# The expert layer of a nine-layer kernel run as one sequence of 128 tiles

## The chip, the cores and the metric

One core of a Trainium2 chip runs the whole program once. The metric is the device time of an execution in microseconds (us). The engines are TensorE (PE in the profile; its weight loads are PEld), VectorE (DVE), ScalarE (ACT), GpSimd (POOL) and SyncE (SP).

## The reference

Input x of 8 x 256 tokens of 128 features goes through four blocks: a block with two quantised attentions and a gated feed-forward, a masked cross attention with a feed-forward, a cross attention, and a decoder block with self attention, cross attention and eight experts. All is float32. The change is in the experts, the last of the nine layers:

```python
def _moe(x, rw, rb, w1, b1, w2, b2):
    ...
    xf = x.reshape(T, D)
    router_weights = jax.nn.softmax(xf @ rw + rb, axis=-1)
    topw, topi = jax.lax.top_k(router_weights, K)          # K = 2 of E = 8
    topw = jax.nn.softmax(topw, axis=-1)
    combine = jnp.zeros((T, E), xf.dtype).at[jnp.arange(T)[:, None], topi].add(topw)
    h = jax.nn.gelu(jnp.einsum('td,edf->etf', xf, w1) + b1[:, None, :], approximate=False)
    eo = jnp.einsum('etf,efd->etd', h, w2) + b2[:, None, :]
    out = jnp.einsum('etd,te->td', eo, combine)
...
x = _layernorm(x + _moe(x, router_w, router_b, e_w1, e_b1, e_w2, e_b2), ln3_g, ln3_b)
```

Every token goes through all eight experts (D = 128, FF = 512), and `combine` weighs them.

## The kernel before

Each engine runs a program of its own, in an order written out by hand; semaphores tie them together. The expert layer takes 2048 tokens as four chunks of 512. A chunk has 32 tiles: tile k is one quarter (128 rows) of the hidden layer of expert k // 4. Float32 is kept by splitting each operand into two float16 parts, hi and lo.

- TensorE, `up` (L1123 to L1125): three matmuls of 512 columns (hi x hi, hi x lo, lo x hi) into one of four PSUM banks. `down` (L1142 to L1144): for each of four token groups three matmuls of 128 columns, gathered over the four tiles of an expert in one of two banks (`TP`). The down of tile k is issued after the up of tile k + 2.
- ScalarE: gelu from the bank to `U_full` in float32 (L1490) and, for three tiles in four, a second pass of the same to the float16 hi part (L1493). Tile k uses slot k % 4.
- VectorE, `split`: the hi part as a cast for k % 4 = 1 (L1962, `HI_BY_VECTOR`), and lo = u - hi for each tile (L1964). `take` (L1974) adds an expert's result, weighed by `combine_down`, to the residual X in four instructions.
- Side work of a chunk. TensorE: transposes of the next chunk's tokens (L1053), the router's matmuls (L1151), the transposes of `combine` (L1159) and the matmuls of the experts' bias (L1165). VectorE: the router's softmax and top 2 as some 24 small dependent instructions (`routing`, parts 0 to 5), statistics and application of the norm for the next chunk (L1515, L1519, L1525) and of the last norm for the chunk before, the tokens and their two float16 parts (`tokens`, `token_parts`), the bias addition (`add_bias`, L1982). GpSimd: two powers for the router (L2449, `route_exp`), inverse deviations (L2196, L2198), scale and shift of the norms (`base` L2205, L2211; `finish` L2386, L2389).
- The token parts have one buffer, rewritten for the next chunk when the last up of the chunk has been issued. The router of the next chunk waits for `routed` 3c + 3, which is the bias addition of this chunk, since both use the PSUM tensor `CO`.

On TensorE and VectorE chunk 0 and chunk 3 are written out and chunks 1 and 2 are a loop; on ScalarE chunks 1 to 3 are a loop. GpSimd's program is written out. GpSimd has also split the expert weights in an earlier layer (L2439).

## Time and profile before

| what | value |
|---|---|
| median of 3 runs | 1049.2 us (1048.2 to 1049.9) |
| the profiled execution's own time | 1049.15 us |
| span of the profile, first to last instruction | 1047.4 us |
| mean granted TensorE clock | 0.862 |
| busy in the span | PE 83%, DVE 73%, ACT 58%, POOL 50% |
| the expert layer's first up | 824.3 us from the span's start |
| its last up matmul | starts at 1034.2 us |

Busy shares are means over nine layers with different limits. For a change in one layer, the layer's own windows and waits are read. A busy time is the union of the records of an engine; records of neighbouring instructions overlap a little, so the distance from a start to the next start is what an instruction costs in a queue.

### The profile page before, as it was taken

To read this page: it belongs to the slowest core of one execution; us is meant where nothing else is said; L and a number is where in the kernel's file an instruction comes from. 1 tells how busy PE (TensorE), PEld (TensorE's weight loads), DVE (VectorE), ACT (ScalarE), POOL (GpSimd) and SP (SyncE) were. 2 spreads that over 40 slices of the span, in tenths; PEclk is the share of its full clock that TensorE was granted. 3 is DMA by queue.
4 is the path that set the end of the run, shared out by engine and by line. 5 is a ranking of instruction groups with operands and counts; after the bars stand their busy time and mean duration, and the time that the engine had idled before them with its cause. 6 is when DMAs were issued, how large, how long until landed. Compare 5 with 4: busy or idle time off the path is not lost.

```text
span 1047.4 us, 23536 instructions
## 1 busy us (share of the span) xinstructions
PE 867.2 (83%) x8314; PEld 528.5 (50%) x8314; DVE 763.5 (73%) x1680; ACT 612.3 (58%) x1487; POOL 519.7 (50%) x1045
## 2 busy tenths in 40 slices
PE   3798888974555877998999799998988788888895
PEld 1344444442333554555765456565555466565664
DVE  5788888978775664565567667677477788989886
ACT  0777777858885313544355456654555566666674
POOL 2677777776563323763444465655244222333313
PEclk9995555555555989999999899999999999999998
DMA  8400000000000000000000010000000000000000
GB/s 266 150 1 2 0 0 1 1 2 0 1 2 0 2 0 1 2 2 2 1 2 2 20 27 22 25 23 15 2 2 2 1 1 2 2 12 0 10 2 21
DMA packets 23573, 16.39 MB, mean 16 GB/s; under 512 B 8744, under 2 KB 20400, under 8 KB 23344
## 3 DMA queue, kind: packets, MB, share of 16 engines
q1 hardware_dynamic: 23472, 15.06, 5.0%
q8 instruction: 61, 1.00, 0.4%
q14 instruction: 40, 0.33, 0.1%
HBM read 10.85 MB, written 1.05 MB: 11 GB/s over the span
## 4 chain that ended last, share of the span: by engine, by line
PE 49%; DVE 25%; ACT 9%; issue 9%; POOL 6%; DMA 1%; DVEq 1%; SPq 0%; ACTq 0%; POOLq 0%
ACT sb_E L1239 5%; PE ps_context L780 5%; DVE sb_neg_raw L1536 3%; PE ps_context L783 3%; POOL sb_E L2261 3%; PE ps_scores L856 3%; DVE sb_E L1964 3%; PE ps_scores L880 3%; DVE sb_inv_den L1779 2%; PE ps_scores L733 2%; PE ps_scores L773 2%; PE ps_turned L1084 2%; PE ps_scores L674 2%; DVE sb_neg_half L1747 2%; PE ps_turned L694 2%
## 5 line engine op out<-in xcount | busy, mean ns | idle before, releaser
L1239 ACT ACTIVATE sb_E<-ps_scores,sb_neg_max,sb_score_scale 128x256 f32<-128x256 f32 (+1 forms) x384 | 190.9, 515 | 64.0 <-DVE sb_neg_max L1539 63.6
L2261 POOL TENSOR_SCALAR sb_E<-sb_E,sb_inv_sum 128x256 f16<-128x256 f32 x256 | 123.6, 483 | 47.3 <-DVE sb_inv_sum L1576 29.5
L1490 ACT ACTIVATE sb_E<-ps_scores,sb_ff_bias 128x512 f32<-128x512 f32 x128 | 87.6, 688 | 66.6 <-PE ps_scores L1125 64.4
L1142 PE MATMUL ps_turned<-sb_moe_down,sb_E 128*128 128x128 f16 x512 | 92.6, 220 | 23.9 <-DVE sb_E L1964 23.8
L1964 DVE TENSOR_TENSOR sb_E<-sb_E 128x512 f16<-128x512 f32 x128 | 93.1, 745 | 23.4 <-ACT sb_E L1493 21.2
L1536 DVE TENSOR_REDUCE sb_neg_raw<-ps_scores 128x4 f32<-128x1024 f32 (+1 forms) x80 | 97.4, 1218 | 14.4 <-PE ps_scores L674 12.0
L1747 DVE TENSOR_REDUCE sb_neg_half<-ps_scores 128x16 f32<-128x1024 f32 x48 | 58.7, 1223 | 67.1 <-PE ps_scores L856 67.1
L1559 DVE TENSOR_REDUCE sb_neg_quad<-ps_scores 128x2 f32<-128x512 f32 (+1 forms) x96 | 64.5, 685 | 42.2 <-PE ps_scores L735 30.1
L1144 PE MATMUL ps_turned<-sb_moe_down,sb_E 128*128 128x128 f16 x512 | 92.1, 219 | 0.0
L1143 PE MATMUL ps_turned<-sb_moe_down,sb_E 128*128 128x128 f16 x512 | 92.1, 219 | 0.0
L2196 POOL TENSOR_SCALAR sb_veps<-sb_mv 128x2 f32<-128x2 f32 x72 | 17.3, 240 | 148.2 <-DVE sb_mv L1519 144.4
L1265 ACT ACTIVATE sb_E<-ps_scores 128x512 f32<-128x512 f32 x96 | 57.0, 598 | 47.7 <-PE ps_scores L775 46.5
L674 PE MATMUL ps_scores<-sb_KBD,sb_QS 32*128 32x512 f16 x128 | 64.2, 602 | 23.5 <-ACT sb_E L1239 15.8
L694 PEld LDWEIGHTS ps_turned<-sb_ident,sb_E 128*128 128x128 f16 x640 | 66.6, 143 | 32.8 <-issue 16.3
L694 PE MATMUL ps_turned<-sb_ident,sb_E 128*128 128x128 f16 x640 | 80.8, 304 | 0.3 <-issue 0.2
L1362 ACT ACTIVATE sb_E<-ps_scores 128x1024 f32<-128x1024 f32 x48 | 49.2, 1024 | 54.5 <-PE ps_scores L888 54.5
L1239 ACT ACTIVATION_READ_ACCUMULATOR sb_E<-ps_scores,sb_neg_max,sb_score_scale 128x1 f32 x384 | 79.7, 207 | 0.0
L1142 PEld LDWEIGHTS ps_turned<-sb_moe_down,sb_E 128*128 128x128 f16 x512 | 50.2, 98 | 50.1 <-DVE sb_E L1964 33.8
L1586 DVE TENSOR_SCALAR sb_VCTX<-ps_turned 128x1024 f16<-128x1024 f16 x80 | 53.7, 672 | 24.6 <-PE ps_turned L694 24.2
L1493 ACT ACTIVATE sb_E<-ps_scores,sb_ff_bias 128x512 f16<-128x512 f32 x96 | 65.4, 681 | 0.0
L2211 POOL TENSOR_TENSOR sb_X<-sb_X,sb_rows 128x256 f32<-128x256 f32 (+1 forms) x64 | 48.1, 752 | 28.7 <-DVE sb_z L1525 26.2
L1779 DVE RECIPROCAL sb_inv_den<-sb_raw_context 128x256 f32<-128x256 f32 x32 | 55.8, 1744 | 4.2 <-ACT sb_raw_context L1370 4.2
(285 smaller groups left out, 2257.2 us busy)
## 6 DMA issues: line engine op xcount, KB each, us to landing
sb_moe_up<-in_moe_up SPq DMA_DIRECT2D x1, 2048.0 KB
sb_KS<-sb_qk_parts SPq DMA_DIRECT2D x96, 16.0 KB, 1.8
sb_QS<-sb_qk_parts SPq DMA_DIRECT2D x96, 16.0 KB, 1.8
sb_rows<-in_rows SPq DMA_DIRECT2D x1, 1216.0 KB, 7.5
out_x<-sb_raw_context SPq DMA_DIRECT2D x8, 128.0 KB, 1.8
sb_X<-in_x SPq DMA_DIRECT2D x1, 768.0 KB, 9.5
sb_square<-in_square SPq DMA_DIRECT2D x1, 768.0 KB, 11.0
sb_ctxT<-in_ctxT SPq DMA_DIRECT2D x1, 512.0 KB, 11.2
```

The costliest lines, as they stand in the source:

```text
L674: last = pe.matmul(dst[:, h:h + 512], QS[group, b, 0, tile:tile + P], KBD[group, b, h:h + 512], start=True, stop=True)
L694: last = pe.transpose(dst[:, P * k:P * k + P], E16[:, ring, P * k:P * k + P], ident16[:, :])
L1142: pe.matmul(dst, u_hi, hi, start=(first and i == 0), stop=False, skip_group_check=True)
L1143: pe.matmul(dst, u_hi, lo, start=False, stop=False, skip_group_check=True)
L1144: last = pe.matmul(dst, u_lo, hi, start=False, stop=final_, skip_group_check=True)
L1239: last = act.activation(E[:, ring, head], SC[t % 2][:, head], ACT.Exp, bias=neg_max[:, ring, h:h + 1], scale=scale, accum_out=row_sum[:, r ...
L1490: last = act.activation(U_full[:, k % 4, :], banks[k % 4], ACT.Gelu, bias=bias, scale=1 / WEIGHT_SCALE)
L1536: dve.tensor_reduce(neg_raw[:, ring, 0:L.heads], src, AX.X, ALU.max).then_inc(S["raw_max"], 1)
L1747: dve.tensor_reduce(neg_half[:, n % 2, :, :, :].rearrange("p x i g -> p (x i g)"), SC[0][:, :].rearrange("p (h k) -> p h k", k=CTX), AX.X, ...
L1779: dve.reciprocal(inv_den[:, :], raw_context[:, x % 2, SEQ:2 * SEQ]).then_inc(S["den_ready"], 1)
L1964: dve.tensor_tensor(lo, u, hi, ALU.subtract).then_inc(S["split"], 1)
L2261: last = pool.tensor_scalar(E16[:, ring, SEQ * h:SEQ * h + SEQ], E[:, ring, SEQ * h:SEQ * h + SEQ], inv_sum[:, ring, h:h + 1], HALF, ALU.m ...
```

## The change

The 128 tiles of the four chunks become one written-out sequence. The down of tile n is issued after the up of tile n + 4 (`BEHIND`), also across chunks. The activations have eight slots (`RING`), the token parts two buffers. Every fourth lo part (k % 4 = 3) is computed by GpSimd (`lower`), with a semaphore of its own. The side work is at other tiles: takes a tile later, the transposes of `combine` from tile 16 to 11, the bias matmuls from 22 to 16, the transposes of the next tokens from 26 to 18, the router from 30 to 25, the bias addition from 27 to 25; statistics and norms one batch at a time; token parts in two steps at tiles 22 and 23; the last norm of the chunk before at tiles 17, 18 (statistics) and 29, 30 (application), where it was at 16 and 20. The buffers are places in tensors that earlier layers have left. The diff, cut to what matters:

```diff
-HI_BY_VECTOR = 1
+HI_BY_VECTOR, LO_BY_POOL = 1, 3
+BEHIND, RING = 4, 8
...
-        h_parts = KBD[:, 0, 0:2 * CHUNK].rearrange("p (s k) -> p s k", s=2)
-        U_parts = E16[:, :, :].rearrange("p r (s k) -> p r s k", s=2)
+        h_parts = KBD[:, 0, 0:4 * CHUNK].rearrange("p (b s k) -> p b s k", b=2, s=2)
+        U_parts = (*(E16[:, i, :] for i in range(4)), *(KBD[:, 1, UNIT * i:UNIT * i + UNIT] for i in range(4)))
         up_parts = moe_up[:, :, :].rearrange("p e k -> p (e k)").bitcast(F16).rearrange("p (e k) -> p e k", e=EXPERTS)
         down_parts = moe_down[:, :, :, :].rearrange("p e t d -> p (e t d)").bitcast(F16)\
             .rearrange("p (e k) -> p e k", e=EXPERTS)
-        U_full = E[:, 2:4, :].rearrange("p r (s k) -> p (r s) k", s=2)
-        final_z = E[:, 0, 0:4 * D].rearrange("p (u t d) -> p u t d", u=2, t=2)
+        U_full = E[:, :, :].rearrange("p r (s k) -> p (r s) k", s=2)
+        final_z = V32[:, 0, :, :, :].rearrange("p t h c -> p (t h c)")[:, 0:4 * D].rearrange("p (u t d) -> p u t d", u=2, t=2)
...
+                    pe.matmul(dst, hi, h_parts[:, c % 2, 0, :], start=True, stop=False)
+                    pe.matmul(dst, hi, h_parts[:, c % 2, 1, :], start=False, stop=False)
+                    pe.matmul(dst, lo, h_parts[:, c % 2, 0, :], start=False, stop=True).then_inc(S["up"], 1)
...
-                    wait(pe, S["split"], B["split"] + n + 1)
+                    if k % 4 == LO_BY_POOL:
+                        pe.wait_ge(S["split_p"], B["split_p"] + n // 4 + 1)
+                    else:
+                        pe.wait_ge(S["split"], B["split"] + n - n // 4 + 1)
...
-                def chunk(c, following):
-                    for k in range(L.tiles):
-                        if not (isinstance(c, int) and c == 0 and k < 2):
-                            up(c, k)
-                        if k == 16:
-                            turn_combine(c)
-                        if k == 22:
-                            expert_bias(c)
-                        if k == 26 and following:
-                            chunk_turn(L, B, c + 1)
-                        if k == 30 and following:
-                            router(c + 1)
-                        if k > 1:
-                            down(c, k - 2)
-                    down(c, L.tiles - 2)
-                    down(c, L.tiles - 1)
+                def tile(n):
+                    c, k = divmod(n, L.tiles)
+                    if n >= 2:
+                        up(c, k)
+                    if k == 11:
+                        turn_combine(c)
+                    if k == 16:
+                        expert_bias(c)
+                    if k == 18 and c < NCHUNK - 1:
+                        chunk_turn(L, B, c + 1)
+                    if k == 25 and c < NCHUNK - 1:
+                        router(c + 1)
...
+                for n in range(NCHUNK * L.tiles + BEHIND):
+                    if n < NCHUNK * L.tiles:
+                        tile(n)
+                    if n >= BEHIND:
+                        down(*divmod(n - BEHIND, L.tiles))
...
+                for n in range(NCHUNK * L.tiles):
+                    k = n % L.tiles
+                    act.wait_ge(S["up"], B["up"] + n + 1)
+                    if n >= RING:
+                        act.wait_ge(S["down"], B["down"] + n - RING + 1)
+                    bias = ff_bias[:, 12 + k:13 + k]
+                    last = act.activation(U_full[:, n % RING, :], banks[n % 4], ACT.Gelu, bias=bias, scale=1 / WEIGHT_SCALE)
+                    if k % 4 != HI_BY_VECTOR:
+                        last = act.activation(U_parts[n % RING][:, 0:CHUNK], banks[n % 4], ACT.Gelu, bias=bias,
                                               scale=1 / WEIGHT_SCALE)
-                        if k % 4 != HI_BY_VECTOR:
-                            last = act.activation(U_parts[:, k % 4, 0, :], banks[k % 4], ACT.Gelu, bias=bias,
-                                                  scale=1 / WEIGHT_SCALE)
-                        last.then_inc(S["act"], 1)
...
-                    wait(dve, S["up"], B["up"] + L.tiles * c)
+                    if c > 1:
+                        dve.wait_ge(S["up"], B["up"] + L.tiles * (c - 1))
                     dve.wait_ge(S["hT_part"], B["hT_part"] + 2 * c + 1)
-                    dve.tensor_copy(h_parts[:, 0, :], h).then_inc(S["hT_part"], 1)
+                    dve.tensor_copy(h_parts[:, c % 2, 0, :], h).then_inc(S["hT_part"], 1)
+                def token_rest(c):
                     dve.wait_ge(S["hT_part"], B["hT_part"] + 2 * c + 2)
-                    dve.tensor_tensor(h_parts[:, 1, :], h, h_parts[:, 0, :], ALU.subtract).then_inc(S["chunk_hT"], 1)
+                    dve.tensor_tensor(h_parts[:, c % 2, 1, :], h, h_parts[:, c % 2, 0, :], ALU.subtract)\
+                       .then_inc(S["chunk_hT"], 1)
                 def split(c, k):
                     n = L.tiles * c + k
                     dve.wait_ge(S["act"], B["act"] + n + 1)
-                    u, hi, lo = U_full[:, k % 4, :], U_parts[:, k % 4, 0, :], U_parts[:, k % 4, 1, :]
+                    u, hi, lo = U_full[:, n % RING, :], U_parts[n % RING][:, 0:CHUNK], U_parts[n % RING][:, CHUNK:]
                     if k % 4 == HI_BY_VECTOR:
                         dve.tensor_copy(hi, u).then_inc(S["u_hi"], 1)
-                        dve.wait_ge(S["u_hi"], B["u_hi"] + L.tiles // 4 * c + k // 4 + 1)
+                        dve.wait_ge(S["u_hi"], B["u_hi"] + n // 4 + 1)
                     dve.tensor_tensor(lo, u, hi, ALU.subtract).then_inc(S["split"], 1)
...
-                def chunk(c, following):
-                    ended = not isinstance(c, int) or c > 0
-                    for k in range(L.tiles):
-                        if k == 28 and following:
-                            tokens(c + 1)
-                        if k == L.tiles - 1 and following:
-                            token_parts(c + 1)
+                def tile(c, k):
+                    following, ended = c < NCHUNK - 1, c > 0
+                    if k % 4 != LO_BY_POOL:
                         split(c, k)
-                        if k == 8 and following:
-                            next_stats(B, c)
-                        if k == 12 and following:
-                            next_norms(B, c)
-                        if k == 30 and following:
-                            routing(c + 1, 0)
-                        if k in (2, 3, 4, 5):
-                            routing(c, k - 1)
-                        if k == 7:
-                            routing(c, 5)
-                        if k == 16 and ended:
-                            final_stats(c - 1)
-                        if k == 20 and ended:
-                            final_norms(c - 1)
-                        if k == 18:
-                            dve.wait_ge(S["logits"], 3 * c + 2)
-                            dve.tensor_copy(combineT[:, :], CO[0:EXPERTS, :]).then_inc(S["routed"], 1)
-                        if k % 4 == 3 and k > 3:
-                            take(c, k // 4 - 1)
-                        if k == 27:
-                            add_bias(c)
-                    take(c, EXPERTS - 1)
+                    if k in (0, 4) and ended:
+                        take(c - 1, EXPERTS - 2 + k // 4)
+                    if k % 4 == 0 and k > 4:
+                        take(c, k // 4 - 2)
+                    if k in (2, 3, 4, 5):
+                        routing(c, k - 1)
+                    if k == 7:
+                        routing(c, 5)
+                    if k in (9, 10) and following:
+                        norm_stats(B, 2 * c + 2 + k - 9, k - 9)
+                    if k == 13:
+                        dve.wait_ge(S["logits"], 3 * c + 2)
+                        dve.tensor_copy(combineT[:, :], CO[0:EXPERTS, :]).then_inc(S["routed"], 1)
+                    if k in (14, 15) and following:
+                        wait(dve, S["x_based"], B["x_based"] + 2 * c + 1 + k - 14)
+                        norm_apply(B, 2 * c + 2 + k - 14, k - 14)
+                    if k in (17, 18) and ended:
+                        final_stats(c - 1, k - 17)
+                    if k == 21 and following:
+                        tokens(c + 1)
+                    if k == 22 and following:
+                        token_parts(c + 1)
+                    if k == 23 and following:
+                        token_rest(c + 1)
+                    if k == 25:
+                        add_bias(c)
+                    if k == 27 and following:
+                        routing(c + 1, 0)
+                    if k in (29, 30) and ended:
+                        final_norms(c - 1, k - 29)
...
+                def lower(n):
+                    u, hi, lo = U_full[:, n % RING, :], U_parts[n % RING][:, 0:CHUNK], U_parts[n % RING][:, CHUNK:]
+                    pool.wait_ge(S["act"], B["act"] + n + 1)
+                    pool.tensor_tensor(lo, u, hi, ALU.subtract).then_inc(S["split_p"], 1)
+                route_exp(0, route[:, 1, :], route[:, 2, :], EXP1)
                 for c in range(NCHUNK):
-                    route_exp(c, route[:, 1, :], route[:, 2, :], EXP1)
-                    route_exp(c, route_s[:, 4, :], route_s[:, 5, :], EXP2)
-                    if c + 1 < NCHUNK:
-                        chunk_norms(L, B, c + 1)
+                    for k in range(LO_BY_POOL, L.tiles, 4):
+                        if k == 7:
+                            route_exp(c, route_s[:, 4, :], route_s[:, 5, :], EXP2)
+                        if k == 11 and c < NCHUNK - 1:
+                            for b in range(2):
+                                inverse_std(B, 2 * c + 2 + b, b)
+                        lower(L.tiles * c + k)
+                        if k == 15 and c < NCHUNK - 1:
+                            for b in range(2):
+                                base(L, B, 2 * c + 2 + b, b)
+                        if k == 19 and c > 0:
+                            final_inverses(c - 1)
+                        if k == 27 and c < NCHUNK - 1:
+                            route_exp(c + 1, route[:, 1, :], route[:, 2, :], EXP1)
                     if c > 0:
                         finish(c - 1)
+                final_inverses(NCHUNK - 1)
                 finish(NCHUNK - 1)
```

## Rows read from the trace of the kernel before

**Rows 1.** The page's part 1, busy time of each engine.

```profile
PE 867.2 (83%) x8314; PEld 528.5 (50%) x8314; DVE 763.5 (73%) x1680; ACT 612.3 (58%) x1487; POOL 519.7 (50%) x1045
```

**Rows 2.** Windows of the expert layer, one row for each chunk.

```profile
core 0: us, PE busy (x) PEld busy (x) DVE busy (x) ACT busy (x) POOL busy (x), PEclk, DMA share, GB/s
...
878.70:933.10 54.40, 46.89 (x509) 32.67 (x507) 47.34 (x128) 35.64 (x56) 19.09 (x19) 1.00 0.02 6
...
987.40:1034.60 47.20, 43.57 (x472) 29.98 (x469) 40.06 (x106) 34.39 (x54) 11.25 (x10) 1.00 0.03 7
```

**Rows 3.** Timeline of TensorE, one tile in step (start, length, line).

```profile
891.55 0.38 PE L1123 MATMUL ps_scores<-sb_KBD,sb_moe_up 128*128 128x512 f16 x1
...
892.20 0.22 PE L1142 MATMUL ps_turned<-sb_moe_down,sb_E 128*128 128x128 f16 x1
...
892.87 0.38 PE L1123 MATMUL ps_scores<-sb_KBD,sb_moe_up 128*128 128x512 f16 x1
```

**Rows 4.** Timeline of TensorE at the router's matmuls.

```profile
928.12 1.05 PE L1151 MATMUL ps_context<-sb_router_w,sb_hT 128*128 128x8 f32 x8 [0.99 <-DVE sb_hT L1945]
929.03 0.22 PE L1142 MATMUL ps_turned<-sb_moe_down,sb_E 128*128 128x128 f16 x1
```

**Rows 5.** Groups of TensorE in chunk 1 (busy us, mean ns, idle before).

```profile
L1165 PE MATMUL ps_context<-sb_moe_b,sb_combineT 8*128 8x128 f32 x8 | 1.2, 283 | 0.0
...
L1053 PE MATMUL ps_rounds<-sb_ident,sb_z 128*128 128x128 f32 x4 | 0.6, 272 | 0.0
```

**Rows 6.** Waits in chunk 1 (us in total, times, longest).

```profile
PE ps_turned L1142 <- DVE sb_E L1964: 7.3, 8, 1.4
...
DVE sb_E L1964 <- ACT sb_E L1493: 4.1, 6, 1.1
```

**Rows 7.** Timeline of all engines, the last tile.

```profile
1034.19 0.38 PE L1125 MATMUL ps_scores<-sb_KBD,sb_moe_up 128*128 128x512 f16 x1
...
1035.19 0.68 ACT L1493 ACTIVATE sb_E<-ps_scores,sb_ff_bias 128x512 f16<-128x512 f32 x1
...
1035.90 0.69 DVE L1964 TENSOR_TENSOR sb_E<-sb_E 128x512 f16<-128x512 f32 x1 [1.22 <-ACT sb_E L1493]
```

**Rows 8.** Timeline of VectorE, chunk 0: routing begins; tiles 24 and 25.

```profile
831.99 0.18 DVE L2042 RECIPROCAL sb_route_s<-sb_route_s 128x4 f32<-128x4 f32 x1
832.20 0.19 DVE L2043 TENSOR_TENSOR sb_route<-sb_route,sb_route_s 128x32 f32<-128x32 f32 x1
...
866.41 0.68 DVE L1964 TENSOR_TENSOR sb_E<-sb_E 128x512 f16<-128x512 f32 x1
867.01 0.42 DVE L1962 CAST sb_E<-sb_E 128x512 f16<-128x512 f32 x1
```

**Rows 9.** VectorE's lo part L1964: the page, then the line's own view.

```profile
L1964 DVE TENSOR_TENSOR sb_E<-sb_E 128x512 f16<-128x512 f32 x128 | 93.1, 745 | 23.4 <-ACT sb_E L1493 21.2
...
L1964 DVE TENSOR_TENSOR sb_E<-sb_E x128: 670/692/1214, 827.9 to 1035.9; 128x512 f16<-128x512 f32 x128
```

**Rows 10.** Groups of VectorE in chunk 1.

```profile
L1519 DVE BATCH_NORM_AGGREGATE sb_mv<-sb_bn 128x2 f32<-128x6 f32 x8 | 1.0, 166 | 0.6 <-DVE sb_bn L1515 0.6
```

**Rows 11.** GpSimd's powers of the router, the line's own view.

```profile
L2449 POOL TENSOR_TENSOR sb_route_s<-sb_euler,sb_route_s x4: 1006/1258/1512, 837.4 to 998.6; 128x4 f32<-128x4 f32 x4
```

**Rows 12.** Timeline of ScalarE, first gelu of chunk 2.

```profile
934.45 0.69 ACT L1490 ACTIVATE sb_E<-ps_scores,sb_ff_bias 128x512 f32<-128x512 f32 x1 [2.64 <-PE ps_scores L1125]
```

**Rows 13.** GpSimd's weight splits L2439, the line's own view.

```profile
L2439 POOL TENSOR_TENSOR sb_moe_up<-sb_act_g,sb_moe_up x8: 1151/1158/1165, 419.7 to 571.4; 128x512 f16<-128x512 f32 x8
```

**Rows 14.** Timeline of VectorE beside GpSimd's residual operations.

```profile
903.06 3.37 DVE L1964 TENSOR_TENSOR sb_E<-sb_E 128x512 f16<-128x512 f32 x3
```

**Rows 15.** Groups of GpSimd before the expert layer (410 to 820 us).

```profile
L2211 POOL TENSOR_TENSOR sb_X<-sb_X,sb_rows 128x256 f32<-128x256 f32 x32 | 23.2, 726 | 4.1 <-DVE sb_z L1525 2.7
```

**Rows 16.** Window of chunk 0 from routing to tile 25.

```profile
831.80:867.00 35.20, 31.13 (x336) 21.30 (x334) 29.96 (x82) 24.13 (x38) 7.98 (x9) 1.00 0.01 1
```

**Rows 17.** Timeline of GpSimd, the last inverse deviations.

```profile
1039.76 0.22 POOL L2196 TENSOR_SCALAR sb_veps<-sb_mv 128x2 f32<-128x2 f32 x1 [15.18 <-DVE sb_mv L1519]
```

More of the change, by code:

```diff
@@ L276, in counts @@
         if layer.experts > 1:
-            c.update(hT_part=2 * NCHUNK, u_hi=n // 4, split=n, chain=NCHUNK * layer.chain, routed=NCHUNK * 3, route_exp=NCHUNK * 2, logits=NCHUNK * 3)
+            c.update(hT_part=2 * NCHUNK, u_hi=n // 4, split=n // 4 * 3, split_p=n // 4, chain=NCHUNK * layer.chain, routed=NCHUNK * 3, route_exp=NCHUNK * 2, logits=NCHUNK * 3)
         return c
@@ L1140, in down @@
                         dst = TP[e % 2][:, P * i:P * i + P]
-                        u_hi, u_lo = (U_parts[:, k % 4, part, P * i:P * i + P] for part in range(2))
+                        u_hi, u_lo = (U_parts[n % RING][:, CHUNK * part + P * i:CHUNK * part + P * i + P] for part in range(2))
                         pe.matmul(dst, u_hi, hi, start=(first and i == 0), stop=False, skip_group_check=True)
@@ L1204, in experts @@
                         plan_step(layer, step)
-                chunk(0, True)
-                with pe.Fori(1, NCHUNK - 1) as c:
-                    chunk(c, True)
-                chunk(NCHUNK - 1, False)
+                for n in range(NCHUNK * L.tiles + BEHIND):
[3 more added lines that the diff above has]
+                        down(*divmod(n - BEHIND, L.tiles))
             pe.wait_ge(loaded["a"], N_LOADS["a"])
@@ L1482, in experts @@
                     act.wait_ge(S[s], B[s])
-                def chunk(c):
-                    for k in range(L.tiles):
-                        n = L.tiles * c + k
-                        act.wait_ge(S["up"], B["up"] + n + 1)
-                        wait(act, S["down"], B["down"] + n - 3)
-                        bias = ff_bias[:, 12 + k:13 + k]
-                        last = act.activation(U_full[:, k % 4, :], banks[k % 4], ACT.Gelu, bias=bias,
-                                              scale=1 / WEIGHT_SCALE)
-                        if k % 4 != HI_BY_VECTOR:
-                            last = act.activation(U_parts[:, k % 4, 0, :], banks[k % 4], ACT.Gelu, bias=bias,
-                                                  scale=1 / WEIGHT_SCALE)
-                        last.then_inc(S["act"], 1)
-                chunk(0)
-                with act.Fori(1, NCHUNK) as c:
-                    chunk(c)
+                for n in range(NCHUNK * L.tiles):
[7 more added lines that the diff above has]
+                        last = act.activation(U_parts[n % RING][:, 0:CHUNK], banks[n % 4], ACT.Gelu, bias=bias,
+                                              scale=1 / WEIGHT_SCALE)
+                    last.then_inc(S["act"], 1)
             act.wait_ge(setup_v, V_SETUP)
@@ L1926, in next_norms, with final_stats, final_norms @@
                     norm_apply(B, 2 * c + 2 + b, b)
-            def final_stats(c):
+            def final_stats(c, b):
                 wait(dve, S["taken"], BASE[-1]["taken"] + EXPERTS * (c + 1))
-                for b in range(2):
-                    norm_stats(Counter(), 2 * c + b, b, sems=fin)
-            def final_norms(c):
-                for b in range(2):
-                    dve.wait_ge(fin["scaled"], 2 * c + b + 1)
-                    norm_apply(Counter(), 2 * c + b, b, sems=fin, z=final_z)
+                norm_stats(Counter(), 2 * c + b, b, sems=fin)
+            def final_norms(c, b):
+                dve.wait_ge(fin["scaled"], 2 * c + b + 1)
+                norm_apply(Counter(), 2 * c + b, b, sems=fin, z=final_z)
             def experts(L, B):
@@ L1979, in add_bias @@
                     dve.wait_ge(S["logits"], 3 * c + 3)
-                    wait(dve, S["taken"], B["taken"] + EXPERTS * c + 6)
+                    wait(dve, S["taken"], B["taken"] + EXPERTS * c + 5)
                     x = chunk_of_x(c)
@@ L2076, in head @@
                         token_parts(c)
+                        token_rest(c)
                     if k == "first":
@@ L2085, in experts @@
                         plan_step(layer, step)
-                chunk(0, True)
-                with dve.Fori(1, NCHUNK - 1) as c:
-                    chunk(c, True)
-                chunk(NCHUNK - 1, False)
-                final_stats(NCHUNK - 1)
-                final_norms(NCHUNK - 1)
+                for c in range(NCHUNK):
+                    for k in range(L.tiles):
+                        tile(c, k)
+                for e in (EXPERTS - 2, EXPERTS - 1):
+                    take(NCHUNK - 1, e)
+                for b in range(2):
+                    final_stats(NCHUNK - 1, b)
+                for b in range(2):
+                    final_norms(NCHUNK - 1, b)
             def chain(sem):
```

9 lines of the change are left out of this document (4 added, 5 removed).

## The prediction

> **What bounds the kernel now.** I read the page first. TensorE is busy 83% of the span and VectorE 73%, so neither is a bound by itself [rows 1]. The diff touches only the expert layer, so the rest of the reading is of that layer. The windows cut it into its four chunks: the first three take 54.4, 54.4 and 54.3 us, the last 47.2, all at a granted clock of 1.00 (the second and the last stand in [rows 2]). In a middle chunk VectorE is busy 47.3 us and idle 7.1; TensorE is busy 46.8, idle 7.5; ScalarE 35.6 and GpSimd 19.1 lie far below. The chunk is longer than either of its two busy engines: they wait for each other in turn.
>
> The timeline of TensorE shows what it needs when nothing is late: from one tile's first up matmul (891.55) to the next (892.87) are 1.32 us, 0.65 for the three ups and 0.67 for the twelve downs [rows 3]. 32 tiles are 42.2 us. Its side work adds about 2.9 us: router 0.91 (928.12 to 929.03), bias matmuls 1.1, two groups of transposes 0.45 each, by issue [rows 4, 5]. So TensorE's floor is 45.1 us a chunk, 9.3 below what it takes.
>
> The waits of a middle chunk say where this goes: TensorE waits for VectorE's lo part (L1964) 7.3 us in 8 places, VectorE for ScalarE 4.1 us in 6 [rows 6]. A down follows its up by only two tiles: from the start of a tile's last up matmul TensorE has 0.22 + 0.67 + 0.65 + 0.67 + 0.65 = 2.9 us of other matmuls before that tile's down. The path through the other engines is: up matmul at 1034.19, second gelu pass ends 1035.87, lo from 1035.90 to 1036.59 [rows 7], 2.4 us. That leaves 0.4 us. Any take (four instructions, 1.04 us) or group of routing links overruns it. Then TensorE stands, its next up is late, and VectorE stands for that up.
>
> **Where the chain goes after the change.** Downs four tiles behind and eight slots let VectorE run 2 x 1.32 = 2.6 us later than now (3.0 in place of 0.4) without stopping TensorE. A short overrun is then absorbed, and the average decides: TensorE's 45.1 against VectorE's load. I make that load from the 47.3 busy of now, term by term.
>
> 1. One lo in four leaves VectorE: 8 of 32 per chunk, each 0.60 us from its start to the next start (866.41 to 867.01 in [rows 8]; the record itself is 0.69 [rows 9]). 47.3 - 4.8 = 42.5. The casts, takes, statistics, norms, links, token parts and bias are the same instructions at other tiles: nothing.
> 2. Gaps that stay: 0.6 between statistics and their aggregate [rows 10], and about 1.0 in some 30 dependent links (0.21 apart at 0.18 busy [rows 8]). 1.6.
> 3. The second exp of the router: GpSimd needs 1.26 in the median [rows 11]. Now two lo parts stand in that gap, afterwards one, since tile 7's lo is GpSimd's. 0.75.
> 4. A wait that moves. The router's matmuls go from tile 30 to 25, and they wait for the bias addition (same PSUM bank, "routed" 3c+3), which goes from 27 to 25. Three tiles of distance become none. At tile 25 TensorE issues the up, then stands until gelu (starts 0.42 after the last up matmul starts [rows 7], one pass, 0.69), cast 0.45, lo 0.60 and addition 0.69 are done: 2.8 us. Behind the router in its queue are down 21 and up 26, so ScalarE and VectorE then find nothing. From the addition's end: router 0.97, down 0.67, two up matmuls 0.43, 0.42 to gelu, two gelu passes 1.27: VectorE idles 3.8 us per chunk. This is the largest price of the change.
> 5. What goes: the stop at the chunk's end. Now the only token buffer is rewritten at tile 31 and TensorE waits for it; ScalarE stood 2.64 us before the next chunk's first gelu [rows 12]. With two buffers this is gone. It is not a term, it is part of the idle time that I don't carry over.
> 6. GpSimd's lo: 128x512 f16 from f32, 1.158 us, in the weight splits, which have exactly this form (8 of the 16 stand in [rows 13]). Eight are 9.3 us a chunk; on 19.1 busy it has room. But it gets in VectorE's way. From 903.06 three lo parts took 3.37 us [rows 14], where 0.60 + 0.60 + 0.69 = 1.9 is the undisturbed time; GpSimd then ran its four 128x256 additions and multiplications of the residual. Over the layer, the mean lo is 745 ns against a median of 692 [rows 9]: 53 ns x 128 = 6.8 us lost. GpSimd has six such groups of four in the layer before the last up, 24 x 0.726 [rows 15] = 17.4 us: 0.39 per us of GpSimd. So 0.45 per moved lo. The bounds: 0 when it runs in VectorE's own gap (tile k%4 = 3 has no lo on VectorE, and in step that leaves 1.3 us for 1.16), and 1.16 when VectorE is behind and always wants the operands. I take 0.45 for six of eight; those of tiles 27 and 31 follow the stop at 25, when VectorE has no backlog. 2.7.
>
> The Trainium skill (SBUF — State Buffer, section "SBUF: two separate sides") says that the pair of ports that VectorE and GpSimd share is an exclusive lock, held for the whole instruction, and that a VectorE instruction with two SBUF inputs takes part in it. The 3.37 us for three agree with it. By that rule a lag on VectorE makes each GpSimd lo cost its full 1.158, which would make rival C of the forecast.
>
> Sum of VectorE's chain: 42.5 + 1.6 + 0.75 + 3.8 + 2.7 = 51.35 us per chunk; TensorE's: 45.1 + 2.8 = 47.9. VectorE sets it, 2.95 below 54.3.
>
> **The sum along the kernel.** Now, VectorE reaches tile 25's cast in chunk 0 at 867.0; its routing of that chunk goes on from 831.8 (the second link after the exp is at 831.99 in [rows 8]). Between, it is busy 30.0 of 35.2 [rows 16]. Six lo parts go (-3.6), tokens and token parts come before tile 25 (+1.8), of 5.2 idle I keep 1.7 (-3.5), contention 6 x 0.45 (+2.7): 864.4, the addition ends 1.75 later, 866.1. Two periods: 968.8. From there no router follows, and TensorE's own chain is the longer: 1.64 to up 26, 37 tiles of 1.32, 0.43, side work 1.6: last up matmul at 1021.3, now 1034.2, so 12.9 us earlier. Tail: the last lo is GpSimd's (+0.56), and the norms of chunk 2 sit at tiles 29, 30, so GpSimd's four multiplications and additions of them (some 3 us) stand before the inverse deviations of chunk 3, which start at 1039.8 now, 5.6 us after the last up matmul [rows 17]: 1.0 late in all. Net 11.9. The profiled execution's own time is 1049.15 (span 1047.4 and 1.75 around it), the median of the runs 1049.2: 1049.15 - 11.9 = **1037.2 us**.
>
> Covered at nothing: other slots in other tiles and unrolled loops (chunk 0 is unrolled and chunk 1 a loop, both 54.4); ScalarE's waits, since it is idle a third of a chunk. Cover for GpSimd's queue: its lo 11 stands behind the inverse deviations of tile 10, about 0.7 to 1.3 us before down 11 needs it; its lo 31 behind the 5.44 us exp. If VectorE is over 1 us behind, TensorE waits there, which costs only what VectorE doesn't have as backlog.
>
> **Rivals.**
> A, TensorE paces: GpSimd's lo falls in VectorE's gaps and costs nothing. Periods of 47.9, chunk 0's addition at 863.4: last up at 1011.7, 22.5 earlier, net 21.5: 1027.7. For it: the gap at every fourth tile. Against: tiles 4 to 7 load VectorE with 7.1 us (three lo parts 1.8, cast 0.45, take 1.04, 14 links 3.1, the wait of term 3) against TensorE's 5.3, and start a lag. 25%.
> B, little is left: contention of about 0.8 on each of the 22 GpSimd lo parts up to tile 25 of chunk 2, 17.6 us where the forecast has 8.1: 1046.7, from 1043 to 1050; or TensorE kept by late GpSimd parts (exp, inverse deviations) while VectorE has no backlog, some 3 us a chunk, to the same sum. For it: the whole routing of tiles 2 to 7 has short instructions that a GpSimd lo of 1.16 can each stop. 19%.
> C, slower: the ports are held for all of each GpSimd lo. Periods 48.65 + 9.3 = 57.9, chunk 0's addition at 870.4, the last part paced by VectorE too (57): last up at 1043, net 10 later: 1059. It decides from about 0.91 us lost per lo, where the 11.9 us are used up (22 x 0.91 = 8.1 + 11.9). Against it: 0.39 per us measured. 8%.
> D, it does not do what it says: TensorE still stops at nearly each take, because up n still needs gelu n-4 (four banks), and the time is as now. Against: by the path above that gelu ends 2.1 us after its up's start, and up n starts 5.3 us after it. 3%.
> Forecast: 45%, own range 1031 to 1043.
>
> **Numbers.** No change is within 0.2% (2.1 us), which is about what the measurement of this kernel can tell. Faster: forecast, A and most of B, 0.87. Same: the end of B and D, 0.05. Slower: C and edges, 0.08. The range runs from A with a somewhat shorter tail (1025) to B with late GpSimd parts (1048).
>
> **What would show it.** Right: middle chunks of 51 to 52 us; one gap of TensorE of 2.8 us or more at the router, once per chunk, and a VectorE gap near 3.8 behind it; no pair of gaps at the chunk's end; the mean VectorE lo above 0.75; 32 GpSimd lo parts between 1.16 and 1.7. Wrong: chunks near 48 with VectorE idle at each fourth tile (A); VectorE lo parts over 0.9 in the mean (B, C); waits of TensorE for GpSimd's lo (B); TensorE waiting for VectorE in eight places a chunk (D).

## The result and the profile after

The changed kernel takes 1061.1 us (median of 4 runs, 1060.6 to 1061.3), the kernel before beside it 1048.7: a ratio of 1.0115, with a 95% interval of 1.010 to 1.013. It is slower by 12 us. The prediction was 1037.2, 12 faster, and the measured time lies outside its range; "slower" had a chance of 0.08.

The windows of the changed kernel, cut at the up of tile 25 of each chunk (columns as in [rows 2]):

```profile
core 0: us, PE busy (x) PEld busy (x) DVE busy (x) ACT busy (x) POOL busy (x), PEclk, DMA share, GB/s
...
864.70:923.50 58.80, 50.60 (x508) 36.61 (x506) 43.25 (x114) 35.91 (x57) 25.12 (x23) 0.91 0.01 1
923.50:981.50 58.00, 49.04 (x508) 35.08 (x506) 45.48 (x118) 35.88 (x57) 29.57 (x27) 0.94 0.02 6
981.50:1045.20 63.70, 56.21 (x593) 40.41 (x591) 46.79 (x119) 42.26 (x67) 24.70 (x20) 0.95 0.02 6
```

A chunk has grown from 54.3 us to 58.8 and 58.0. VectorE is busy 43.3 and 45.5 us of it, about the 45.2 that the forecast gives it (42.5 + 2.7). But it is idle 12.5 to 15.5 us, where the forecast has 6. And the granted clock of TensorE, 1.00 in every chunk before, is 0.91 to 0.95. The waits of the first of these windows show whom TensorE waits for, to be set against [rows 6]:

```profile
PE ps_context L1155 <- DVE sb_X L1983: 4.2, 1, 4.2
...
PE ps_context L1163 <- DVE sb_combine L2073: 1.5, 1, 1.5
...
PE ps_turned L1146 <- POOL sb_E L2467: 1.4, 1, 1.4
...
PE ps_context L1169 <- DVE sb_combineT L2003: 0.9, 1, 0.9
...
PE ps_turned L1146 <- DVE sb_X L1975: 0.2, 1, 0.2
```

The eight short waits for VectorE's lo part are gone, as the deeper sequence promised. In their place stand four long ones, of which three are side work: the router (L1155) for the bias addition, the transposes of `combine` (L1163) for `combine`, the bias matmuls (L1169) for its copy, and one down (L1146) for GpSimd's lo. Around the first router, on TensorE and on VectorE:

```profile
864.68 0.38 PE L1124 MATMUL ps_scores<-sb_KBD,sb_moe_up 128*128 128x512 f16 x1
...
869.70 1.85 PE L1155 MATMUL ps_context<-sb_router_w,sb_hT 128*128 128x8 f32 x8 [4.21 <-DVE sb_X L1983]
871.40 0.27 PE L1146 MATMUL ps_turned<-sb_moe_down,sb_KBD 128*128 128x128 f16 x1
...
872.63 0.63 PE L1124 MATMUL ps_scores<-sb_KBD,sb_moe_up 128*128 128x512 f16 x1
...
875.20 0.63 PE L1124 MATMUL ps_scores<-sb_KBD,sb_moe_up 128*128 128x512 f16 x1
```

```profile
864.72 1.53 DVE L1954 TENSOR_TENSOR sb_KBD<-sb_hT,sb_KBD 128x512 f16<-128x512 f32 x1
866.17 0.68 DVE L1965 TENSOR_TENSOR sb_E<-sb_E 128x512 f16<-128x512 f32 x1
866.78 1.12 DVE L1975 SCALAR_TENSOR_TENSOR sb_X<-ps_turned,sb_combine_down,sb_X 128x128 f32<-128x128 f32 x4
867.81 0.41 DVE L1963 CAST sb_E<-sb_E 128x512 f16<-128x512 f32 x1
868.26 0.69 DVE L1965 TENSOR_TENSOR sb_E<-sb_E 128x512 f16<-128x512 f32 x1
868.87 0.68 DVE L1983 TENSOR_TENSOR sb_X<-ps_context,sb_X 128x512 f32<-128x512 f32 x1
875.53 0.69 DVE L1965 TENSOR_TENSOR sb_E<-sb_E 128x512 f16<-128x512 f32 x1 [5.97 <-ACT sb_E L1494]
```

Between the up of tile 25 (864.68) and that of tile 26 (872.63) are 8.0 us, between 26 and 27 another 2.6, where 1.32 is the pace [rows 3]. TensorE stands 4.2 us; then everything that it does takes twice as long: the router 1.70 from start to next start (0.91 in [rows 4]), an up matmul's record 0.63 (0.38), the down 1.23 (0.67). VectorE, which TensorE has waited for, gets its next lo at 875.53, after 6.0 us of idle. The clock in that stretch:

```profile
865.00:868.00 3.00, 0.49 (x3) 0.00 (x0) 3.00 (x7) 1.17 (x2) 0.70 (x1) 1.00 0.00 0
868.00:869.00 1.00, 0.00 (x0) 0.00 (x0) 0.97 (x3) 0.00 (x0) 0.00 (x0) 1.00 0.00 0
869.00:870.00 1.00, 0.30 (x2) 0.33 (x2) 0.55 (x1) 0.00 (x0) 0.00 (x0) 0.66 0.00 0
870.00:876.00 6.00, 6.00 (x37) 4.67 (x37) 0.47 (x1) 1.27 (x2) 0.00 (x0) 0.50 0.01 3
876.00:877.00 1.00, 1.00 (x15) 0.83 (x14) 0.70 (x4) 0.49 (x1) 0.00 (x0) 0.93 0.00 0
```

It falls from 2.4 to 1.2 GHz at about 869.3, near the end of the gap, and returns at about 876.1.

### The profile page after: what moved, and what is told of

It reads as the page before. It is cut to its first block, busy times and chain, and to the rows that moved or that the text cites. A ratio compares the mean times of both kernels' runs of the same rounds, so it can differ in the third digit from the quotient of the medians.

```text
span 1059.4 us, 23096 instructions
## 1 busy us (share of the span) xinstructions
PE 874.6 (83%) x8314; PEld 536.4 (51%) x8314; DVE 755.1 (71%) x1648; ACT 612.4 (58%) x1487; POOL 558.7 (53%) x1077
## 4 chain that ended last, share of the span: by engine, by line
PE 48%; DVE 27%; issue 9%; ACT 9%; POOL 6%; DMA 1%; DVEq 0%; SPq 0%; POOLq 0%; ACTq 0%
ACT sb_E L1241 5%; PE ps_context L781 5%; DVE sb_neg_raw L1534 3%; PE ps_context L784 3%; POOL sb_E L2271 3%; PE ps_scores L857 3%; PE ps_scores L881 3%; DVE sb_inv_den L1777 2%; DVE sb_X L1975 2%; PE ps_scores L734 2%; PE ps_scores L774 2%; PE ps_turned L1085 2%; PE ps_scores L675 2%; DVE sb_neg_half L1745 2%; PE ps_scores L1069 1%
## 5 line engine op out<-in xcount | busy, mean ns | idle before, releaser
L1965 DVE TENSOR_TENSOR sb_E<-sb_E 128x512 f16<-128x512 f32 x48 | 38.4, 808 | 26.6 <-ACT sb_E L1494 25.7
L2208 POOL TENSOR_TENSOR sb_rstd<-sb_veps,sb_minus_half 128x2 f32<-128x2 f32 x72 | 53.1, 738 | 6.0
L1146 PE MATMUL ps_turned<-sb_moe_down,sb_KBD 128*128 128x128 f16 x256 | 50.2, 230 | 2.0 <-DVE sb_X L1975 1.0
L1146 PE MATMUL ps_turned<-sb_moe_down,sb_E 128*128 128x128 f16 x256 | 46.2, 219 | 5.7 <-POOL sb_E L2467 4.3
L1148 PE MATMUL ps_turned<-sb_moe_down,sb_KBD 128*128 128x128 f16 x256 | 50.2, 230 | 0.0
L1147 PE MATMUL ps_turned<-sb_moe_down,sb_KBD 128*128 128x128 f16 x256 | 50.2, 230 | 0.0
```

The costliest lines, as they stand in the source:

```text
L1146: pe.matmul(dst, u_hi, hi, start=(first and i == 0), stop=False, skip_group_check=True)
```

## The experiments

All are edits of the changed kernel, timed beside the kernel before in several rounds. Ratios are to the kernel before.

### The bias addition earlier, alone

```diff
-                    wait(dve, S["taken"], B["taken"] + EXPERTS * c + 5)
+                    wait(dve, S["taken"], B["taken"] + EXPERTS * c + 3)
...
-                    if k == 25:
+                    if k == 19:
                         add_bias(c)
```

> The bias addition of a chunk goes from tile 25 to tile 19 (it then waits for three takes, not five); all else is as in the changed kernel. Theory S (the router's matmuls stop TensorE at tile 25 because the addition that they wait for has the same tile; the step from up 25 to up 26 is 8.0 us, the next 2.6, against 1.3 each; the granted clock halves in it): the stop goes, three times 7.9 us or a little less, 1061 to about 1039 to 1043. Theory G (GpSimd's lo parts take VectorE's operand ports, VectorE is behind, and TensorE waits wherever it next asks): the wait goes elsewhere, at most 6 us are won, 1055 or more.

1039.7 us, ratio 0.990 (0.988 to 0.992): 21.4 us less than the changed kernel. Six tiles between the addition and the router turn a loss of 12 into a gain of 10. Theory S had 1039 to 1043 and holds; G had 1055 or more.

```profile
865.80:915.40 49.60, 45.60 (x508) 33.20 (x506) 43.25 (x115) 35.85 (x57) 25.44 (x23) 1.00 0.01 2
915.40:967.90 52.50, 47.74 (x508) 34.15 (x506) 45.49 (x119) 35.85 (x57) 28.88 (x27) 0.97 0.02 6
```

The chunks are 49.6 and 52.5 us long with the same busy time on VectorE. The step to up 26 is 2.1 us. So the stop and what follows it cost 21 us of the kernel, and no other wait takes their place.

### The stop left in, but TensorE kept busy in it

```diff
-BEHIND, RING = 4, 8
+BEHIND, RING, WARM = 4, 8, 16
...
                 def router(c):
                     wait(pe, S["hT_part"], B["hT_part"] + 2 * c + 1)
+                    if c > 0:
+                        for _ in range(WARM):
+                            pe.matmul(RD[:, :], up_parts[:, 0, 0:P], up_parts[:, 1, 0:CHUNK], start=True, stop=True)
                     wait(pe, S["routed"], 3 * c)
```

> The changed kernel with 16 idle matmuls of 512 columns (some 3.5 us, result unused, written to the PSUM bank of the turned tokens after those were read) put before TensorE's wait for the bias addition at tile 25. The wait itself stays. If the halved clock is a part of the cost: router, down 21 and the next two ups run at full clock, 1.35 + 1.25 us less for each of three routers, 1061 to about 1053. If the stop alone costs, and the clock's fall is only its companion: 1061.

1050.8 us, ratio 1.001 (1.000 to 1.002): 10.3 less, with 48 useless matmuls more in the program.

```profile
863.42 0.38 PE L1124 MATMUL ps_scores<-sb_KBD,sb_moe_up 128*128 128x512 f16 x1
...
864.07 3.62 PE L1155 MATMUL ps_rounds<-sb_moe_up 128*128 128x512 f16 x16
868.34 1.06 PE L1158 MATMUL ps_context<-sb_router_w,sb_hT 128*128 128x8 f32 x8 [0.66 <-DVE sb_X L1986]
...
869.92 0.38 PE L1124 MATMUL ps_scores<-sb_KBD,sb_moe_up 128*128 128x512 f16 x1
...
871.24 0.38 PE L1124 MATMUL ps_scores<-sb_KBD,sb_moe_up 128*128 128x512 f16 x1
...
872.14 0.69 DVE L1968 TENSOR_TENSOR sb_E<-sb_E 128x512 f16<-128x512 f32 x1 [3.85 <-ACT sb_E L1497]
```

The idle matmuls (3.62) fill the gap, the router starts no earlier behind up 25 (4.9 us, 5.0 without them), but it and all that follows run at full clock: up 26 comes 6.5 us after up 25 and not 8.0, up 27 another 1.32 after and not 2.6. VectorE's idle time behind the addition is 3.85 us and not 6.0. The two steps save 2.8 us at each of three routers, 8.4 in all. The rest of the 10.3 is not shown: the ten runs lie between 1048.5 and 1053.0, and in the profiled one (1053.0) the layer is 7.1 us shorter than in the changed kernel, since the clock now falls for 3.4 us at another place (963.9). So the halved clock alone is 8 to 10 of the 21.4 us that the stop costs. The page TensorE: Matmul & The Clock Gate of the Trainium skill (Part 1) calls the two levels cold and warm and puts the fall down to idleness; these runs agree, with a gap of 4.2 us on one side and idle matmuls in the same gap on the other. The last section has a fall without one long gap.

### All lo parts on VectorE

```diff
-                    if k % 4 == LO_BY_POOL:
-                        pe.wait_ge(S["split_p"], B["split_p"] + n // 4 + 1)
-                    else:
-                        pe.wait_ge(S["split"], B["split"] + n - n // 4 + 1)
+                    pe.wait_ge(S["split"], B["split"] + n + 1)
...
-                    if k % 4 != LO_BY_POOL:
-                        split(c, k)
+                    split(c, k)
...
-                        lower(L.tiles * c + k)
```

> The changed kernel with all lo parts on VectorE again, none on GpSimd. Theory G: each lo on GpSimd costs VectorE as much as it saves or more, and TensorE's waits for GpSimd's lo go too: 1050 or less. Theory S: VectorE has 13 to 15 us of idle in a chunk and its load is not what sets the time; 4.8 us more work in a chunk against waits of 3 us that vanish: 1058 to 1066.

1050.7 us, ratio 1.002 (1.001 to 1.004): 10.3 less. Here G (1050 or less) comes close and S (1058 to 1066) fails, the other way round from `bias19`: each theory names one of two causes. S did not see that GpSimd's lo could cost through single places. One of them, in the changed kernel and in this run, is the first link behind the router's second power (`[...]` is the idle time before it):

```profile
896.83 1.11 DVE L2068 TENSOR_SCALAR sb_route_s<-sb_route_s 128x4 f32<-128x4 f32 x1 [0.90 <-POOL sb_route_s L2461]
```

```profile
893.42 0.17 DVE L2064 TENSOR_SCALAR sb_route_s<-sb_route_s 128x4 f32<-128x4 f32 x1 [0.30 <-POOL sb_route_s L2457]
```

A tensor_scalar of four elements for each of 128 rows takes 1.11 us beside GpSimd's lo 7 (896.77 to 897.92) and 0.17 without. `combine` comes that much later, and TensorE waits for just that. The step to up 16, at which TensorE waited for GpSimd's lo 11, falls from 2.9 to 1.3 us.

### The depth undone

```diff
-BEHIND, RING = 4, 8
+BEHIND, RING = 2, 8
```

> The changed kernel with the down two tiles behind the up in place of four, slots still eight. If the depth does its part (in the changed kernel some twenty steps of a chunk are at 1.32 us): every take stops TensorE again as in the kernel before, 3 to 4 us a chunk more, 1070 to 1078. If the depth is worth nothing: 1061.

1067.9 us, ratio 1.018 (1.016 to 1.020): 6.8 more than with four tiles. The depth is worth having even here, though less than expected (1070 to 1078): the large stops hide some of the small ones. TensorE's gap before the router is 3.6 us and not 4.2, the step to up 26 is 6.1 to 6.9 and not 8.0.

### More distance in the side work, with GpSimd's lo and without

```diff
-                    if k == 11:
+                    if k == 13:
                         turn_combine(c)
-                    if k == 16:
+                    if k == 19:
                         expert_bias(c)
...
-                    if k == 13:
+                    if k == 15:
                         dve.wait_ge(S["logits"], 3 * c + 2)
...
-                    if k == 25:
+                    if k == 22:
                         add_bias(c)
```

(The addition then waits for four takes.) 

> The changed kernel with more tiles between what TensorE waits for and the wait: transposes of combine at tile 13 (VectorE makes combine at 7), its copy at 15, bias matmuls at 19, bias addition at 22, router still at 25. Theory S (each stop of TensorE in its own queue costs its length, since the up behind it is late too): beyond the run with the addition at 19 (1039.7), the 2.2 us before up 12 and the 2.2 us before up 17 of each chunk go, the stop of 1.6 us for GpSimd's lo 11 stays: some 4 x 4 less, 1022 to 1028. Theory V (VectorE's load sets the time once the stops are gone, 48.6 us or more a chunk with the contention, as forecast): 1034 to 1040.

1042.3 us, ratio 0.994 (0.992 to 0.996). Theory S fails, and V's range (1034 to 1040) is missed too: the stops at 12 and 17 are gone, but 16 us are not won against `bias19`: nothing is (1042.3 against 1039.7). Others have come: in a middle chunk the step to up 13 is 3.2 us, and that to up 26 is 3.7 in place of 2.1, since the router waits 1.3 us for an addition that is only three tiles ahead. (The 2.5 us to up 20 are no stop; the bias matmuls now stand there.) At 13:

```profile
887.21 1.12 DVE L2068 TENSOR_SCALAR sb_route_s<-sb_route_s 128x4 f32<-128x4 f32 x1 [0.90 <-POOL sb_route_s L2461]
...
888.36 0.23 PE L1146 MATMUL ps_turned<-sb_moe_down,sb_KBD 128*128 128x128 f16 x1 [0.42 <-POOL sb_KBD L2467]
...
891.53 0.22 PE L1146 MATMUL ps_turned<-sb_moe_down,sb_E 128*128 128x128 f16 x1 [1.69 <-DVE sb_X L1975]
```

VectorE's link again takes 1.12 beside GpSimd's lo 7; the down of that tile waits for GpSimd; the link and the lo behind it are late, so is the take, and TensorE waits for the take's bank (891.53, 1.69 us idle).

The same with the edit of `lo_vector` on top: 

> The same as the run named spread, with all lo parts on VectorE. Theory S: the stop for GpSimd's lo 11 goes (1.6 us a chunk) and so does the lock on VectorE's operands; VectorE then has 47 us of work in a chunk against 45 of TensorE: 1020 to 1027, as the run spread or a little better. Theory V: 4.8 us more a chunk on the engine that is the bound: 1045 or more.

1028.3 us, ratio 0.981 (0.978 to 0.983). V (1045 or more) fails, S (1020 to 1027) comes close. This is the fastest version of the study, 21 below the kernel before, 33 below the changed one.

```profile
862.90:909.90 47.00, 45.62 (x508) 33.22 (x506) 43.32 (x124) 35.88 (x57) 15.94 (x14) 1.00 0.01 2
909.90:958.10 48.20, 45.80 (x508) 33.00 (x505) 45.43 (x128) 35.81 (x57) 19.71 (x18) 1.00 0.03 7
```

In the second row VectorE is busy 45.4 and TensorE 45.8 of 48.2 us, at full clock. GpSimd's lo parts cost 14 us here.

### GpSimd's order, and a dose of the stop

In `spread2` GpSimd computes lo 11 before the inverse deviations. What follows from these moves too: by one or two tiles on VectorE and TensorE, by one lo part, which is four tiles, on GpSimd:

```diff
+                        lower(L.tiles * c + k)
                         if k == 11 and c < NCHUNK - 1:
                             for b in range(2):
                                 inverse_std(B, 2 * c + 2 + b, b)
-                        lower(L.tiles * c + k)
```

> The run spread, and GpSimd computes its lo 11 before the inverse deviations and not behind them; what follows from these moves on with it (norms at tiles 15 and 16, transposes of the next tokens at 20, tokens and their parts at 22 to 24, base after lo 19, last inverse deviations after lo 23). Theory S: the 1.6 us before up 16 go too, 6 less than spread, 1016 to 1022. If VectorE or GpSimd is the bound by then: as spread.

1039.4 us, ratio 0.991 (0.989 to 0.993), 3 less than `spread`, half of what was expected. The step to up 16 falls from 2.4 to 1.3 us as meant, but that to up 13 grows from 3.2 to 4.0. The order of GpSimd's queue is a small part of the cost of its lo.

In `bias24` only the addition moves, from tile 25 to 24: 

> The changed kernel with the bias addition at tile 24 behind the take, in place of 25: a stop of TensorE of about 3.2 us at the router in place of 4.2. If the clock halves only behind the longer stop: the step to up 26 takes about 5.5 us and the next 1.3, 3 x 3.7 less than 1061, 1050. If it halves here too: 6.9 and 2.6, 1058.

1055.6 us, ratio 1.007 (1.004 to 1.009): 5.5 less, nearer to the second case. In its trace the steps to up 26 are 7.1, 6.0 and 7.1 us and those to 27 are 2.6: the gap before the router is 3.3 us and not 4.2, and that does not keep the clock.

### GpSimd's subtractions that nobody needs

`spread_lo`, and GpSimd computes at the old places 32 subtractions of the same form on data at rest, into a tile that nobody reads:

```diff
-                    u, hi, lo = U_full[:, n % RING, :], U_parts[n % RING][:, 0:CHUNK], U_parts[n % RING][:, CHUNK:]
+                    u, hi, lo = act_g[:, 1, :], up_parts[:, 0, 0:CHUNK], act_g[:, 0, :].bitcast(F16)[:, 0:CHUNK]
                     pool.wait_ge(S["act"], B["act"] + n + 1)
+                    wait(pool, S["split_p"], B["split_p"] + n // 4)
                     pool.tensor_tensor(lo, u, hi, ALU.subtract).then_inc(S["split_p"], 1)
```

> The run spread_lo (all lo parts on VectorE, 1028.3), and GpSimd computes beside it, at the times at which it computed its lo parts, 32 subtractions of the same form on data that nothing else touches, into a tile that nobody reads. Nobody waits for them, the output is unchanged. Theory P (GpSimd's lo costs by holding operands back from VectorE): VectorE loses 0.4 to 1.16 us by each, it has no room left, 1040 to 1060. Theory Q (it cost because TensorE waited for GpSimd's result, late in GpSimd's queue): 1028.

1047.3 us, ratio 0.998 (0.996 to 0.999): 19 us more than `spread_lo`, for work that touches no tile of VectorE and that nobody waits for. So theory P holds: they cost by their presence. 19 / 32 is 0.59 us each. The layer as a whole, first of `spread_lo`, then of this run (columns as above):

```profile
825.20:1013.10 187.90, 179.29 (x1950) 127.81 (x1950) 169.80 (x466) 142.28 (x223) 62.29 (x52) 1.00 0.02 4
```

```profile
825.50:1031.20 205.70, 185.00 (x1950) 130.09 (x1950) 190.87 (x465) 142.33 (x223) 105.52 (x83) 0.98 0.01 4
```

VectorE has the same instructions (one record is missing) and is busy 190.9 us in place of 169.8, 0.66 more for each subtraction. Its waits for GpSimd are the same in both (1.5, 1.2 and 1.0 us in the whole layer), so it is not that GpSimd's other results come later. Groups of VectorE, first of `spread_lo`, then of this run (busy, mean ns):

```profile
L1962 DVE TENSOR_TENSOR sb_E<-sb_E 128x512 f16<-128x512 f32 x48 | 34.0, 721 | 3.2 <-ACT sb_E L1491 2.2
...
L1960 DVE CAST sb_KBD<-sb_E 128x512 f16<-128x512 f32 x12 | 5.0, 418 | 0.1
```

```profile
L1962 DVE TENSOR_TENSOR sb_E<-sb_E 128x512 f16<-128x512 f32 x47 | 36.0, 779 | 2.6 <-ACT sb_E L1491 2.0
...
L1960 DVE CAST sb_KBD<-sb_E 128x512 f16<-128x512 f32 x12 | 6.3, 521 | 0.1
...
L2064 DVE TENSOR_SCALAR sb_route_s<-sb_route_s 128x4 f32<-128x4 f32 x3 | 3.4, 1122 | 0.9 <-POOL sb_route_s L2457 0.9
```

This lo goes from 721 to 779 ns in the mean, the cast from 418 to 521, and the link of tile 7 takes 1.12 us.

### Two parts undone at once, the depth again, and still more distance

`bias19_lo` has the edits of `bias19` and of `lo_vector`: 

> The changed kernel with two of its parts undone at once: bias addition at tile 19 (alone 1039.7, 21.3 less than the changed kernel) and all lo parts on VectorE (alone 1050.7, 10.3 less). If the two are separate causes: 1061.1 - 21.3 - 10.3 = 1029.5. If they share one cause (VectorE's lag at the router): 1036 or more.

1030.7 us, ratio 0.982 (0.979 to 0.984). The two causes add up: 1061.1 - 21.4 - 10.3 = 1029.4, and 1030.7 is measured.

`spread_lo_b2` is `spread_lo` with `BEHIND` of 2: 

> The run spread_lo with the down two tiles behind the up. The depth's own worth, with the stops and GpSimd's lo out of the way: if VectorE's overruns stop TensorE as in the kernel before, 4 to 6 us a chunk, 1044 to 1052; if depth is worth little next to the double token buffer and the spread: 1030 to 1036.

1046.0 us, ratio 0.996 (0.995 to 0.998). With the stops and GpSimd's lo out of the way the depth is worth 17.7 us; without it, nearly all of the gain is gone. `wide` has all lo parts on VectorE and the side work further apart (transposes at 15, copy 17, bias matmuls 21, addition 24, router 27, first links of the next chunk 29): 

> All lo parts on VectorE, and still more distance than in spread_lo: transposes of combine at 15, copy at 17, bias matmuls at 21, addition at 24, router at 27, first routing links of the next chunk at 29. The stops of 1.6 us before up 13 and 1.7 and 1.2 before ups 19 and 20 may go; but a chunk of 48.2 us has VectorE busy nearly throughout. If VectorE is now the bound: 1025 to 1029. If the stops are: 1018 to 1022.

1030.7 us, ratio 0.982 (0.980 to 0.984). Both expectations are missed, and more distance than in `spread_lo` brings nothing. In a middle chunk TensorE still waits 1.4 us for the bank of a take, 0.9 before the transposes of the next tokens and 0.5 at the router; in `spread_lo` it is 1.4 and 1.0 in the first two places. VectorE and TensorE are both busy 45.8 of the 49 us of the second middle chunk. Whether one of them or the waits are then the bound no run shows.

## Why the prediction was wrong

The step that failed is the sum, "VectorE sets it, 2.95 below 54.3". The load of VectorE came out (45.2 forecast, 45.5 measured in a middle chunk with all side work), but by luck: two errors cancel. `spread_lo` needs 45.4 in the same chunk with all 32 lo parts, so without eight of them 40.6 and not 42.5; GpSimd's eight put back 4.9 and not 2.7. And this load sets a period only if VectorE always has work, where the forecast let one idle of 3.8 us stand beside it. TensorE's stops made it idle 12.5 to 15.5 us. TensorE sets the period: 45.1 of its own, 9.0 of waits in the second middle chunk where the forecast had one of 2.8, and 2.8 for the halved clock are 56.9 of the 58.0. Against 1037.2, the measured 1061.1 is 23.9 more. From the traces: the first addition ends at 869.55 and not 866.1 (+3.4, of which 0.8 is a later start of the layer); two periods from addition to addition are 58.8 and 58.0 and not 51.35 each (+14.1); from the last router to the last up matmul (1045.67) are 59.3 and not 52.5 us (+6.8); the tail is 13.8 and not 14.2 (-0.4). By cause:

- **Term 4, the wait that moves.** Its place and kind were right: TensorE stands at the router and down 21 and up 26 stand behind it. Its size was not. 2.8 us, counted from the start of the last up matmul, were worked out for a VectorE that has nothing else to do; so counted, 4.6 are measured (865.11 to 869.70), of which TensorE is idle 4.2. VectorE still had lo 24 and the take of tile 24 before the cast, and ahead of them the second token part, which took 1.53 in place of 0.69 beside GpSimd's lo 23. That VectorE then idles 6.0 in place of 3.8 is not this term's fault: with the clock kept, in `warm`, it is 3.85.
- **No term for the clock.** [rows 2] have 1.00 throughout, and the forecast carried this over to a kernel that it gave a new gap in each chunk. `warm` puts it at 8.4 us by its steps and 10.3 by its time. This is the largest omission.
- **Term 1, "the same instructions at other tiles: nothing".** The transposes of `combine` and the bias matmuls were moved with fewer tiles of distance (from nine tiles behind `combine` to four, from four behind the copy to three), and no wait was costed at either. They stop TensorE for 1.5 and 0.9 us in the first middle chunk; the steps there are 3.4 and 4.0 us. No run undoes these two alone; in `spread` they go and others come.
- **Term 6, GpSimd's lo.** The mechanism was right, the mean too small: 0.45 of VectorE's time for each, against 0.66 in `shadow`. It does its harm in the time of the kernel where VectorE stands on a path that TensorE waits for. Taking it out wins 10.3 us in the changed kernel and 14 in `spread`. That it would relieve VectorE, 4.8 us a chunk, was booked in full. Over the layer VectorE is busy 168.2 us in the changed kernel and 170.3 in `lo_vector`, which has 32 lo parts more on it, 19.2 us at 0.60. Of the relief 2.1 us arrived, half a microsecond a chunk.
- **Cover.** "Its lo 11 about 0.7 to 1.3 us before down 11 needs it" was too little: TensorE waits 1.4 us there.

Rival C, the slower one (1059), came out near in time, but not as it was worked out: it had chunks of 57.9 by VectorE's load. Blocking for nearly the whole length happens, yet not at all eight: in chunk 1 a VectorE instruction is lengthened by 0.84 to 0.98 us beside GpSimd's lo 7, 11, 15, 23 and 31, and by next to nothing beside the other three. The Trainium skill (SBUF — State Buffer, section "Who interferes with whom") adds that casts and tensor_scalar can take the shared ports too; the link of 0.17 us that takes 1.11 and the cast of 0.42 that reaches 1.34 agree.

What was right: the stop at the chunk's end is gone (the steps from up 30 to up 35 are at 1.32), the eight waits for VectorE's lo too, the depth works (6.8 us as changed, 17.7 cleaned up), GpSimd's lo takes 1.158 in the median (up to 1.60), VectorE's lo 0.77 in the mean, the wait of term 3 is 0.90 for 0.75, and the tail is later by 0.6 us where 1.0 was given.

## What to carry to other kernels

When an order of side work is changed, list each wait of the in-order engine with the number of tiles between it and what it waits for; a distance that shrinks to zero is a stop in every round, and its length is the whole path through the other engines with their backlog, not without it. Where such a stop is new, ask what the clock does behind it, even if it never fell before. And before work is given to a helper engine beside a nearly full one, the same instructions can be tried as idle work: 32 that nobody needed cost 19 us here.

## What the runs showed of the hardware that was not expected

- One gap of TensorE of 4.2 us was followed by 6.8 us at 1.2 GHz (windows above), three times in the changed kernel, and idle matmuls in the gap prevented it. A gap of 3.3 us (`bias24`) did not keep it either. The kernel before has waits of up to 1.55 us in the layer, and its clock did not fall there.
- The clock also fell without one long gap: in the first middle chunk near 910.3, for 3.4 us, behind two waits of 1.4 and 0.9 us that lie 2.4 us apart, and for as short a stretch in several of the other runs. In the next chunk the same two waits (966.3 and 968.7) were followed by no fall; what decides it is not shown.
- GpSimd's two-input subtraction of 1.16 us held up a VectorE instruction with a single small input (0.15 to 0.17 us alone, 1.12 beside it) for most of its length.
- The same subtractions, on data that nothing else used, made VectorE's busy time 21 us longer (`shadow`).
